# VectorE evicts the next batch's transposes in front of splitting the stacks (first attention of a two-layer block)

## The reference, cut to what matters

```
h = layernorm(x) * (1 + ca) + sa              # modulation per batch
x_norm = layernorm(h) * gamma + beta
q, k = x_norm @ w_q, x_norm @ w_k ; v = h @ w_v     # 16 heads of 8
q, k = q / |q|, k / |k|
resonance = 0.5 + 0.5 * tanh((q.k - 0.27) * 15)
gate_q, gate_k = 0.25 + 0.75 * sigmoid(q.g_q), 0.25 + 0.75 * sigmoid(k.g_k)
x = x + ga * (((resonance * gate_q * gate_k) @ v) @ w_o + b_o)
```

## Time and profile before

| What | us |
|---|---|
| Median of 3 runs | 1505.26 (1504.54 to 1508.08) |
| The profiled execution, its own time | 1505.55 |
| Its span, first to last instruction | 1503.7 |
| First attention, in the span | 20 to 446 |
| DVE busy over the span | 1139.2 (76%) |
| PE busy over the span | 1280.3 (85%) |
| ACT busy over the span | 933.0 (62%) |

### The profile page before, as it was taken

One profiled execution on the slowest core, in us unless ns is written; L12 is line 12 of the kernel. 1 busy time (PEld: TensorE's weight loads), 2 busy tenths in 40 slices (PEclk: granted clock), 3 DMA queues, 4 the chain that ended last, 5 costly groups with the idle time before them and its releaser, 6 DMA issues. The chain is left out here.

```text
span 1503.7 us, 37667 instructions
## 1 busy us (share of the span) xinstructions
PE 1280.3 (85%) x12442; PEld 827.7 (55%) x12442; DVE 1139.2 (76%) x3067; ACT 933.0 (62%) x1292; POOL 550.9 (37%) x771
## 2 busy tenths in 40 slices
PE   2688888888876877778758999999965999999998
PEld 1454455554533635454535555555533777777776
DVE  3799999999847575857568999999945677777763
ACT  0488888888872323232416888888864666766675
POOL 1233333333414131312113333333303656655653
PEclk6699999999998989998978999999986999999999
DMA  3311111111001010100020000000000000000000
GB/s 79 143 33 32 31 33 37 34 31 31 18 10 44 9 36 9 32 11 15 15 85 12 13 13 14 14 14 13 12 7 0 8 7 14 14 14 7 14 14 23
DMA packets 44734, 37.50 MB, mean 25 GB/s; under 512 B 5136, under 2 KB 43472, under 8 KB 44144
## 3 DMA queue, kind: packets, MB, share of 16 engines
q1 hardware_dynamic: 44656, 36.50, 8.3%
HBM read 32.14 MB, written 4.34 MB: 24 GB/s over the span
## 5 line engine op out<-in xcount | busy, mean ns | idle before, releaser
L1966 ACT ACTIVATE a_probs<-psum_all 128x1024 f32<-128x1024 f32 x256 | 248.1, 1022 | 86.8 <-PE psum_all L1881 86.8
L474 ACT ACTIVATE probs<-psum_all,biases 128x1024 f32<-128x1024 f32 x256 | 270.6, 1112 | 44.2 <-PE psum_all L385 43.4
L2354 PE MATMUL psum_all<-ffn_hi,weights_r 128*128 128x512 f32 x704 | 286.6, 407 | 8.2 <-POOL ffn_lo L2314 4.9
L2354 PE MATMUL psum_all<-ffn_lo,weights_r 128*128 128x512 f32 x704 | 280.5, 398 | 0.0
L2314 POOL TENSOR_TENSOR ffn_lo<-ffn_full,ffn_hi 128x512 fp32r<-128x512 f32 x144 | 189.7, 1326 | 126.7 <-ACT ffn_hi L2439 87.6
L2354 PEld LDWEIGHTS psum_all<-ffn_hi,weights_r 128*128 128x128 f32 x704 | 133.5, 190 | 50.0 <-DVE ffn_full L2569 8.7
L2354 PEld LDWEIGHTS psum_all<-ffn_lo,weights_r 128*128 128x128 f32 x704 | 134.2, 191 | 28.6
L398 PE MATMUL psum_all<-probs,vpad 128*32 128x257 f32 x2048 | 139.1, 389 | 0.3 <-ACT probs L474 0.3
L1895 PE MATMUL psum_all<-a_probs,vpad 128*32 128x256 f32 x2048 | 137.9, 387 | 0.1
L2451 ACT ACTIVATE ffn_full<-psum_all,scales 128x512 f32<-128x512 f32 x128 | 88.2, 689 | 70.2 <-PE psum_all L2354 69.9
L2314 DVE TENSOR_TENSOR ffn_lo<-ffn_full,ffn_hi 128x512 fp32r<-128x512 f32 x64 | 55.0, 860 | 80.5 <-ACT ffn_hi L2454 80.5
(11 more groups left out here) (223 smaller groups left out, 2776.9 us busy)
## 6 DMA issues: line engine op xcount, KB each, us to landing
a_mod_gate<-modulation_table SPq DMA_DIRECT2D x64, 128.0 KB, 2.9
a_mod_norm<-modulation_table SPq DMA_DIRECT2D x32, 128.0 KB, 3.0
X<-in_x SPq DMA_DIRECT2D x32, 128.0 KB, 2.9
f<-in_f SPq DMA_DIRECT2D x2, 2048.0 KB, 10.0
e_mod_norm<-modulation_table SPq DMA_DIRECT2D x32, 128.0 KB, 2.9
out<-X SPq DMA_DIRECT2D x16, 256.0 KB, 2.3
e_gates<-modulation_table SPq DMA_DIRECT2D x32, 64.0 KB, 2.7
weights<-in_h SPq DMA_DIRECT2D x2, 1024.0 KB, 7.7
```

What stands on the lines that cost most here:

```text
L474: nc.scalar.activation(probs[:, c % 4, :, :, 0:T].rearrange("p r k q -> p (r k) q"), SC[c % 2].rearrange("p (a q) -> p a q", q=T), ACT.Tan ...
L1966: nc.scalar.activation(probs[:, c % 4, :, :, :].rearrange("p r k q -> p (r k q)"), SC[c % 2], ACT.Exp, scale=float(np.float32(1.0) / np.sq ...
L2354: ins = nc.tensor.matmul(dst, weights[:, w0:w0 + P], part[layer][:, k, :], start=first and i == 0, stop=last and i == len(parts) - 1)
```

## The change

In DVE's step, the eviction of batch b+2's transposes is taken from the head of the step. In its place, the eviction of batch b+3's transposes (the same work, one step earlier in the pipeline) stands between `gate_sums(b+2)` and `split_high(b+2)`. The buffer that it writes is the same as before: batch b+3 goes to `hT[1 - p]`. It waits, as before, for `turned` and for `vl_psum` (the projections that read the last hT and xnT). No other engine's code changes.

```
@@ step(b, p) of VectorE
-                if next_:
-                    turned_out(b + 2, p)
                 if ahead:
                     stats_1(b + 3)
                 if older:
...
                 if next_:
                     scale(b + 2)
                     gate_sums(b + 2)
+                if ahead:
+                    turned_out(b + 3, 1 - p)
+                if next_:
                     split_high(b + 2, p)
                     split_low(b + 2, p)
```

## The result

The changed kernel takes 1481.5 us (median of 4 runs, 1481.14 to 1481.86) against 1505.12 for the kernel before in the same series: ratio 0.984, 95% interval 0.982 to 0.986. That is 23.6 us less, where 20 were forecast; 1481.5 lies in the stated range.

What follows compares the result with a forecast made beforehand. In the first attention, DVE's queue plus mutual waits of DVE and PE (xnT, value projection) was taken to set the step. Savings of 15.9 + 2.7 + 1.6 = 20.2 us gave 1485 us, range 1476 to 1498.

Steps and rivals of the forecast that it cites:

- The ring and what goes: First attention: PE's 1.38 us wait for xnT, DVE's at values and ACT's 0.51 and 0.62 all go.
- The root behind it: At xhat, DVE would newly wait for POOL's reciprocal root, 0.33 us per step (bounds 0.27 to 0.45).
- The wait for the transposes: At the moved hT eviction, DVE would newly wait 0.14 us per step for PE's transposes, paid in full.
- The step: Steady first attention: 0.73 - 0.14 = 0.59 us saved, 12.14 becomes 11.55; 15.9 us over 27 steps.
- the clock case: Rival: no fall to the lower clock in the first attention, total 1483.5 us; chance 0.08.
- The first steps: Start of first attention, PE at half rate: gains of 1.4 and about 1.3 us, together 2.7.
- The tail: End of the first attention, where the last projection waits 2.02 us: gain 1.6 us, bounds 1.0 to 2.0.
- The rest of the kernel: Everything behind the first attention was to keep its length and start 20 us earlier.
- The bigger wait: Rival: another hand-over, such as heads waiting for heads_out, starts to bind; half the steady gain, 1494 us; chance 0.18.
- Slower: Rival: late transposes hold DVE in front of the splits for more than 0.73 us; 1514 us; chance 0.07.
- No new waits: Rival: DVE's waits for POOL's root and PE's transposes are absent or tiny; 1472 us; chance 0.08.
- no change: Rival: PE reaches the transposes 0.6 us after xn, so DVE waits the 0.73 it gained; 1505 us; chance 0.07.

Runs made afterwards that it cites:

- evict_first: Changed kernel with the eviction one place further ahead, right behind norm_2b, in front of scale and gate_sums: 1504.8 us, ratio 1.000 to the kernel before.
- before_xhat_ahead: Kernel before, eviction where it was, with norm_1b moved in front of values and logits_out: 1506.3 us, ratio 1.000 to the kernel before.
- changed_again: The changed kernel as it is, run once more for a second profile: 1481.2 us, ratio 0.984 to the kernel before.
- pad_before_stats: Changed kernel with one added 128x128 memset on VectorE per step in front of stats_1: 1483.8 us.
- pad_before_xhat: Changed kernel with one added 128x128 memset on VectorE per step in front of norm_1b: 1481.2 us.

## Why the prediction was right, step by step

*The ring and what goes.* Right. PE's wait at L328, DVE's at L684 and ACT's at its squares are gone, and ACT idles longer at a step's first chunk, as forecast (1.04 against 0.39 in the steps shown).

*The root behind it.* Right: 0.33 forecast, 9.0 / 27 = 0.33 measured, and shown as a real term by three runs (a pad vanishes in it, a pad elsewhere doesn't, starting the root earlier removes it). From aggregates to xhat I had taken 1.34 from the first steps; it is 1.40.

*The wait for the transposes.* Forecast 0.14, measured 1.36 - 1.29 = 0.07. This error and the 0.06 of the root cancel: that the step came out at 11.55 to the hundredth is partly luck. That such a wait is paid in full was shown by `evict_first`.

*The step.* Forecast 11.55, measured 11.55 to 11.56. The 27 steps give 17.7 instead of 15.9, and the difference is the fall of the clock that the changed kernel doesn't have. This is the clock case. Both profiles of the kernel before have such a fall between 68 us and the end of the stage, worth some 1.6 and 2.4 us. None of the nine profiles with the early eviction has one, but neither has that of `before_xhat_ahead`, where PE's idle time at L328 is as long as ever. So the early eviction may make it rarer; it isn't shown.

*The first steps.* The term that was mis-sized: 2.7 forecast, 5.4 measured. The first two steps gave 1.4 and 1.5, as worked out. The third, 15.05 before, took 12.48, and I had counted nothing for it. Part is that the early eviction helps it too, and part is the clock. It stood at 1.2 GHz until about 66 us before, and until about 58 us in the changed kernel, in whose window from 56 to 60 us the mean is 0.72:

```profile
56.00:60.00 4.00, 4.00 (x43) 2.69 (x44) 2.71 (x12) 2.90 (x4) 1.62 (x3) 0.72 0.01 4
60.00:64.00 4.00, 3.68 (x59) 1.74 (x58) 3.67 (x16) 3.74 (x5) 2.85 (x5) 1.00 0.31 91
```

In `changed_again` and `pad_before_stats` it returned at about 59 us, and their third steps, from xnT to xnT, took 12.12 and 11.96, against 11.98 in the first profile. In `pad_before_xhat` it returned at about 64 us, and there this step took 13.12. So 1.1 of the 2.6 us that it gave goes with the moment of the return. The other 1.4 are not the change's alone, since the kernel before stayed at 1.2 GHz for 2 us longer still; at the price of these runs, 1.1 for 6 us, that would be 0.4 (an estimate), and 1.0 would be left for the change. Nor does the moment look like mere chance: with the early eviction the clock came back between 58 and 64 us in nine profiles, without it between 65 and 67 us in three. Without it PE starts the third projection at 56 to 58 us instead of 54 to 56. Whether the earlier work brings the clock back earlier, no run separates.

*The tail.* 1.6 forecast, 1.1 measured.

*The rest of the kernel.* I had it unchanged; it took 1.4 more, and 0.8 less stood in front of the stage. Both are of the size by which equal kernels differ here: from the expert layer's first instruction to the end the two profiles of the kernel before took 1057.2 and 1056.1, those of the changed kernel 1058.6 and 1056.3.

*The rivals.* The bigger wait has a trace: `heads` does wait for `heads_out` in 16 steps, 0.26 each, the margin that I had called near zero. It seems to cost nothing, since PE then waits 0.41 for xn anyway. "Slower" was a real mechanism at a place nearby: with the eviction one place further ahead the whole gain is lost. "No new waits" is refuted by the waits, and "no change" by PE's idle 0.41 in front of the transposes: it isn't late for them.

## What to carry to other kernels

When a wait is removed from a queue, look for what was hidden in it: here another engine's root, whose chain gives back 0.33 of 0.98 us, and which a swap of two lines then recovers. Put an eviction behind just as much independent work as its producer takes, and an independent instruction between a writer and its reader. And before moving work of VectorE in time, see which instructions of GpSimd it would then meet.

## What the runs showed of the hardware that I had not expected

- A VectorE instruction that waits for the semaphore of the one right in front starts 0.45 us behind the start of a 0.42 us one, an independent one 0.34: the dependence costs 0.11 us, and the table of waits doesn't show it.
- An added VectorE memset of 0.17 us lengthens the queue by 0.08 to 0.09.
- VectorE instructions of 0.2 us at the least last 0.73 (median of L609 in `before_xhat_ahead`) where they meet a GpSimd pass; moving one by a few tenths moved 0.3 us per step in or out.
- The return from 1.2 to 2.4 GHz at the start came between 58 and 64 us with the early eviction (nine profiles) and between 65 and 67 us without it (three); the same order of work gave 58 and 59, with one memset more 59 and 64.
